# A 15 by 15 box filter's second layer: rows turned through one scaled difference instead of two products

## The reference

```python
x = x + mean_filter(group_norm(x), k=15)   # ones/15 down the rows, then ones/15 along them, zero padding of 7
```

## Time and profile before

| | us |
|---|---|
| median of 3 runs (3734.6 to 3736.6) | 3735.91 |
| the profiled execution | 3737.8 |
| its span | 3736.0 |
| TensorE busy in the span | 3338.8 (89%) |
| VectorE busy | 3140.5 (84%) |
| GpSimd busy | 2583.7 (69%) |
| ScalarE busy | 2201.5 (59%) |
| layer 1 of the second image, 914 to 1073 | 159 |

### The profile page before, as it was taken

The page is one execution under the profiler, slowest core; times in us unless marked ns, Lnnn a source line. Parts: engine busy times, 40 slices in busy tenths (PEclk is TensorE's granted clock), DMA queues, the critical chain, the costliest instruction groups (busy, mean ns, idle before and its releaser), DMA issues.

```text
span 3736.0 us, 114624 instructions
## 1 busy us (share of the span) xinstructions
PE 3338.8 (89%) x38496; PEld 2215.3 (59%) x38496; DVE 3140.5 (84%) x5910; ACT 2201.5 (59%) x4341; POOL 2583.7 (69%) x2119
## 2 busy tenths in 40 slices
PE   2199899998989989899899998999899998999978
PEld 1155476555765567555675556755576555765567
DVE  6689977998879978899788997789877998879976
ACT  2778733786248852588426883278633786248842
POOL 4089952997639965499546995389853996639964
PEclk9599999999999999999999999999999999999999
DMA  9566577664867648666485665766477664866634
GB/s 212 167 103 129 98 198 189 118 129 83 237 159 126 128 96 238 140 126 128 123 238 116 127 122 153 222 107 128 96 202 188 119 128 85 236 160 125 129 85 136
DMA packets 720201, 544.18 MB, mean 146 GB/s; under 512 B 589840, under 2 KB 665200, under 8 KB 707568
## 3 DMA queue, kind: packets, MB, share of 16 engines
q1 hardware_dynamic: 697456, 422.30, 51.5%
q10 hardware_dynamic: 22400, 117.46, 11.8%
HBM read 258.41 MB, written 148.90 MB: 109 GB/s over the span
## 4 chain that ended last, share of the span: by engine, by line
PE 77%; DVE 8%; issue 5%; ACT 4%; SPq 2%; ACTq 1%; DMA 1%; POOL 1%; DVEq 0%; POOLq 0%
PE p L581 24%; PE h_ps L693 15%; PE h_ps L491 9%; PE h_odd L491 9%; PE p L719 6%; PE p L530 5%; PE p L588 3%; PE h_ps L581 2%; DVE ob_all L1295 2%; ACT arena L762 1%; ACTq L920 1%; PE p L499 1%; PE h_ps L588 1%; SPq L413 1%; ACT ob_all L783 1%
## 5 line engine op out<-in xcount | busy, mean ns | idle before, releaser
L581 PE MATMUL p<-arena,bd_all 64*64 64x512 f16 x16896 | 1291.2, 381 | 33.2 <-DVE ob_all L1217 23.2
L1427 POOL TENSOR_TENSOR arena<-img 128x512 f32<-128x512 f32 x392 | 499.5, 1275 | 459.4 <-PE h_ps L693 437.8
L762 ACT ACTIVATE arena<-h_ps 128x512 f16<-128x512 f32 x512 | 305.8, 597 | 834.9 <-PE h_ps L693 596.3
L581 PEld LDWEIGHTS p<-arena,bd_all 64*64 64x64 f16 x16896 | 552.5, 105 | 379.5 <-issue 240.0
L1378 POOL TENSOR_TENSOR ob_all<-ob_all,img 128x512 f32<-128x512 f32 x512 | 663.5, 1296 | 91.1 <-DVE ob_all L1211 62.7
L1381 POOL TENSOR_TENSOR ob_all<-ob_all 128x512 f32<-128x512 f32 x512 | 653.4, 1276 | 40.1
L693 PE MATMUL h_ps<-bd_all,arena 128*128 128x128 f32 x3584 | 539.5, 286 | 0.0
L1279 DVE TENSOR_TENSOR arena<-h_ps,arena 128x512 f16<-128x512 f32 x512 | 353.3, 690 | 209.4 <-ACT arena L762 207.8
L693 PEld LDWEIGHTS h_ps<-bd_all,arena 128*128 128x128 f32 x3584 | 447.6, 191 | 121.2 <-issue 115.8
L1211 DVE SCALAR_TENSOR_TENSOR ob_all<-p,bias_c,cosw 128x256 f32<-128x256 f32 x1024 | 447.6, 478 | 59.8 <-PE p L581 23.0
L837 ACT ACTIVATE img<-img,half_row (+1 forms) x1024 | 486.4, 528 | 4.7
(11 more groups left out here) (177 smaller groups left out, 5050.9 us busy)
## 6 DMA issues: line engine op xcount, KB each, us to landing
out<-ob_all SPq DMA_DIRECT2D x512, 256.0 KB, 4.2
bd_all<-bd_dram SPq DMA_DIRECT2D x512, 224.0 KB, 2.6
img<-in_x ACTq DMA_DIRECT2D x168, 512.0 KB, 7.2
img<-in_x ACTq DMA_DIRECT2D x112, 256.0 KB, 4.7
img<-in_x SPq DMA_DIRECT2D x24, 512.0 KB, 25.7
bd_dram<-ob_all SPq DMA_DIRECT2D x11, 768.0 KB, 4.9
arena<-arena SPq DMA_TRANSPOSE x512, 2.8
xT_more<-arena SPq DMA_TRANSPOSE x512, 2.8
```

The lines of the kernel that those rows point to most:

```text
L581: m = mm(bank[out_half * HP:(out_half + 1) * HP, :], bd[s % RB][rows, 6 * lm + (j if own else j + 1), :], part, start=opens and i3 == 0, s ...
L1427: G.tensor_tensor(diff[u % 2], img[:, u + R, :], img[:, u - R - 1, :], ALU.subtract).then_inc(moved, 1)
```

## The change

Every row from 1 to 63 is now one difference. For u = 1 to 7 the upper neighbour's rows 57 to 63, and for u = 57 to 63 the lower neighbour's rows 0 to 6, are copied by DMA one band over into seven buffers `across` (`rows_before` and `rows_after`, issued by SyncE; the outermost band gets zeros from the table `no_row`). GpSimd subtracts for all 63 rows. ScalarE scales the difference in place (`scale_row`), with a bias for the outermost bands in the 14 border rows, and no scaled matrices are made. TensorE turns the scaled row with its transpose instruction in f32, identity as the moving operand, into one of four banks, two rows ahead of the box instead of one. `parts` and `diff` have three buffers instead of two. The waits of GpSimd's first differences are on the copies (`before_in`) and no longer on `s_scale`. `border`, `kept_row` and the product that spread the mean (line 730) are gone. A load of the next image waits for seven more differences than before.

```diff
@@ -51,7 +51,9 @@
 SCRATCH = 16
-NDIFF = T - K
+NDIFF = T - 1
+NTURN = 4
+COPIES = 5
 LAG = 16
@@ -181,10 +184,14 @@
-        diff = [piece[s] for s in range(2)]
-        parts = [piece[2 + s].bitcast(F16).rearrange("p (l k m) -> p l k m", l=2, k=NQ) for s in range(2)]
+        diff = [piece[s] for s in (0, 1, 11)]
+        parts = [piece[s].bitcast(F16).rearrange("p (l k m) -> p l k m", l=2, k=NQ) for s in (2, 3, 12)]
         head, tail = piece[14], piece[15]
-        kept_row = [piece[4 + r] for r in range(R - 1)] + [head]
+        across = [piece[4 + r] for r in range(R)]
+        across_all = arena[:, 4 * W:(4 + R) * W]
+        def diff_row(u):
+            return across[u - 1] if u <= R else diff[u % 3] if u < T - R else across[u - (T - R)]
@@ -238,7 +242,8 @@
         c_tab = h_ps[:, 1, 0:3 * P].rearrange("p (i t a) -> p i t a", i=3, a=2)
-        turned_ps = [h_ps[:, s, :].rearrange("p (k m) -> p k m", k=NQ) for s in range(2)]
+        turned_ps = [bank.rearrange("p (k m) -> p k m", k=NQ)
+                     for bank in (h_ps[:, 0, :], h_ps[:, 1, :], h_odd[:], p1[:])]
@@ -429,19 +433,49 @@
+            def rows_before(b):
+                def shifted(first, rows, signal):
+                    to, at = across_all[:, first * W:(first + rows) * W], T - R + first
+                    of = img[:, at:at + rows, :].rearrange("p t w -> p (t w)")
+                    for hl in range(HL - 1):
+                        sp.dma_start(to[hl + 1:P:HL], of[hl:P:HL]).then_inc(signal, 16)
+                    sp.dma_start(to[HP:P:HL], of[HL - 1:HP:HL]).then_inc(signal, 16)
+                sp.wait_ge(p0_ready, (b + 1) * T + PRIMED)
+                sp.dma_start(across_all[0:HP:HL], tab["no_row"]).then_inc(before_in[0], 16)
+                sp.wait_ge(x1_whole, (b + 1) * T - 3)
+                shifted(0, 4, before_in[0])
+                sp.wait_ge(x1_whole, (b + 1) * T)
+                shifted(4, 3, before_in[1])
+            def rows_after(b):
+                of = img[:, 0:R, :].rearrange("p t w -> p (t w)")
+                sp.wait_ge(turned, b * T + R + 1)
+                for hl in range(HL - 1):
+                    sp.dma_start(across_all[hl:P:HL], of[hl + 1:P:HL]).then_inc(after_in, 16)
+                sp.dma_start(across_all[HL - 1:HP:HL], of[HP:P:HL]).then_inc(after_in, 16)
+                sp.dma_start(across_all[HP + HL - 1:P:HL], tab["no_row"]).then_inc(after_in, 16)
             with sp.Fori(0, B - 1) as b:
                 matrices(b)
+                rows_before(b)
                 for j in range(T // 2):
...
                     store(b, j, j % NS)
+                    if j == 2:
+                        rows_after(b)
                     if j == 4:
...
@@ -687,27 +721,23 @@
-                def turn_row(u, *terms):
+                def turn_first():
                     for k in range(NQ):
-                        for i, (mat, row) in enumerate(terms):
-                            m = mm(turned_ps[u % 2][:, k, :], row[:, k * P:(k + 1) * P], mat,
-                                   start=(i == 0), stop=(i == len(terms) - 1))
+                        cols = slice(k * P, (k + 1) * P)
+                        mm(turned_ps[0][:, k, :], head[:, cols], tb["ident"][:], start=True, stop=False)
+                        m = mm(turned_ps[0][:, k, :], tail[:, cols], tb["prev"][:], start=False, stop=True)
                     m.then_inc(turned, 1)
...
-                    if u >= 2:
-                        pe.wait_ge(low_done, b * T + u - 1)
-                    if u <= R:
-                        turn_row(u, (turn_mat["ident"], img[:, u + R, :]),
-                                 (turn_mat["neg_prev"], img[:, u + T - R - 1, :]))
-                    elif u < T - R:
-                        pe.wait_ge(moved, b * NDIFF + u - R)
-                        turn_row(u, (turn_mat["ident"], diff[u % 2]))
-                    else:
-                        pe.wait_ge(row_kept, b * R + u - (T - R) + 1)
-                        turn_row(u, (turn_mat["next_"], kept_row[u - (T - R)]),
-                                 (turn_mat["neg_ident"], img[:, u - R - 1, :]))
+                    if u >= NTURN:
+                        pe.wait_ge(low_done, b * T + u - (NTURN - 1))
+                    pe.wait_ge(scaled_row, b * NDIFF + u)
+                    for k in range(NQ):
+                        m = nc.tensor.transpose(turned_ps[u % NTURN][:, k, :], diff_row(u)[:, k * P:(k + 1) * P],
+                                                tb["ident"][:])
+                    m.then_inc(turned, 1)
@@ -716,7 +746,7 @@
                         for l in range(2):
-                            m = mm(p0[0][:, lo:hi], parts[u % 2][:, l, k, :],
+                            m = mm(p0[0][:, lo:hi], parts[u % 3][:, l, k, :],
                                    tb["band16"][:, lo - k * P + R:hi - k * P + R],
@@ -725,15 +755,11 @@
                 pe.wait_ge(tail_ready, b + 1)
-                turn_row(0, (tb["ident"][:], head[:]), (tb["prev"][:], tail[:]))
-                pe.wait_ge(mean_made, b + 1)
-                mm(c_ps[:, 24:24 + C], sc[:, 24:25].broadcast_to([P, P]), mean_in[:], start=True, stop=True).then_inc(mean_spread, 1)
-                pe.wait_ge(mats_ready, b * 4 + 2)
+                turn_first()
+                turn_step(1)
                 for u in range(T):
-                    if u + 1 < T:
-                        if u + 1 == T - R:
-                            pe.wait_ge(mats_ready, b * 4 + 4)
-                        turn_step(u + 1)
+                    if u + 2 < T:
+                        turn_step(u + 2)
                     box_row(u)
@@ -895,35 +921,39 @@
+                def scale_row(u):
+                    act.wait_ge(moved, b * NDIFF + u)
+                    bias = edge_bias[:, 0:1] if u <= R else edge_bias[:, 1:2] if u >= T - R else None
+                    scaled(diff_row(u), diff_row(u), sc[:, 10:11], bias).then_inc(scaled_row, 1)
                 def high_part(u):
-                    if R < u < T - R or u == 0:
-                        act.wait_ge(turned, b * T + u + 1)
-                    else:
-                        act.wait_ge(bordered, b * (2 * R) + (u if u <= R else u - (T - R) + R + 1))
-                    if u >= 2:
-                        act.wait_ge(banded, b * T + u - 1)
-                    copy(parts[u % 2][:, 0], turned_ps[u % 2]).then_inc(high_done, 1)
+                    act.wait_ge(turned, b * T + u + 1)
+                    if u >= 3:
+                        act.wait_ge(banded, b * T + u - 2)
+                    copy(parts[u % 3][:, 0], turned_ps[u % NTURN]).then_inc(high_done, 1)
...
                 scaled(head, head, sc[:, 10:11], sc[:, 18:19]).then_inc(head_ready, 1)
-                scaled(turn_mat["ident"], tb["ident"][:], sc[:, 10:11]).then_inc(mats_ready, 1)
-                scaled(turn_mat["neg_prev"], tb["prev"][:], sc[:, 17:18]).then_inc(mats_ready, 1)
+                act.wait_ge(ends_ready, b + 1)
+                scale_row(1)
+                scale_row(2)
                 high_part(0)
-                scaled(turn_mat["next_"], tb["next_"][:], sc[:, 10:11]).then_inc(mats_ready, 1)
-                scaled(turn_mat["neg_ident"], tb["ident"][:], sc[:, 17:18]).then_inc(mats_ready, 1)
                 def load_next(t, rows, signal):
...
                     act.wait_ge(row_out, PRIMED + b * T + t + rows)
-                    if t + rows <= NDIFF:
-                        act.wait_ge(moved, b * NDIFF + t + rows)
+                    if t + rows + R <= NDIFF:
+                        act.wait_ge(moved, b * NDIFF + t + rows + R)
+                    if t < R:
+                        act.wait_ge(after_in, (b + 1) * (16 * COPIES))
                     for i in range(2):
...
                 for u in range(1, T):
+                    if u + 2 < T:
+                        scale_row(u + 2)
                     high_part(u)
-                    if u <= R:
-                        copy(kept_row[u - 1], img[:, u - 1, :]).then_inc(row_kept, 1)
                     if follow:
@@ -1276,16 +1306,8 @@
                     dve.wait_ge(high_done, b * T + u + 1)
-                    V.tensor_tensor(parts[u % 2][:, 1], turned_ps[u % 2], parts[u % 2][:, 0],
+                    V.tensor_tensor(parts[u % 3][:, 1], turned_ps[u % NTURN], parts[u % 3][:, 0],
                                     ALU.subtract).then_inc(low_done, 1)
-                def border(u):
-                    dve.wait_ge(turned, b * T + u + 1)
-                    first, op = (0, ALU.add) if u <= R else (HP + HL - 1, ALU.subtract)
-                    edge_cols = turned_ps[u % 2][:, :, first:first + HP - HL + 1:HL]
-                    V.tensor_tensor(edge_cols, edge_cols, mean_row[:].unsqueeze(1).broadcast_to([P, NQ, C]),
-                                    op).then_inc(bordered, 1)
@@ -1298,16 +1320,13 @@
                 V.tensor_scalar(tail, tail, sc[:, 10:11], sc[:, 23:24], ALU.mult, ALU.add).then_inc(tail_ready, 1)
```

(39 more changed lines are left out.)

18 lines of the change are left out of this document (9 added, 9 removed).

## The result

The changed kernel takes 3852.03 us (median of 4 runs, 3848.83 to 3856.55) against 3735.28 before (4 runs, 3734.6 to 3736.6): 1.0315 times as long, 95% interval 1.0302 to 1.0328. Forecast were 3607, in a range from 3540 to 3690, so a faster kernel; this one is slower.

What follows compares the result with a forecast made beforehand. TensorE was taken as the bound nearly everywhere. Savings of 9.6 + 10.5 + 0.7 - 3.5 - 2.4 = 14.9 us an image, by seven 104, plus 25.0 in the last, gave 129 off 3737.8: 3607 us, range 3540 to 3690.

Steps and rivals of the forecast that it cites:

- The step that failed: Rows 17 to 55: GpSimd, at 1.28 us a difference plus a quarter of a table product, was not the bound.
- four candidates for rows 17 to 55: Possible next bounds per row: VectorE 1.81 us, GpSimd 1.28 plus a quarter table product, ScalarE 1.69, transfers 1.83 or 1.91.
- Rival 3: Layer 1's rows: TensorE's clock falls if transpositions do not hold it up; 4180 us; 9%, plus 4% for some rows only.
- the turn at 0.53 us: TensorE's turning of a row by transposition takes 0.53 us, where the f32 product took 1.05.
- rows without sums at 1.55: Rows 0 to 17 and the last image: 1.55 us a row, 9.6 us saved in rows 0 to 17.
- the last image: Row 0 to row 63 falls from 125.1 to 97.7 us through more banks, buffers and lead; 25.0 saved after the start.
- the start 2.4 late: Before row 0: three two-input VectorE instructions computing the scale each wait 0.8 us behind GpSimd's differences, 2.4 us an image.
- rival 2: Before row 0: all small scale instructions alternate with GpSimd's differences, start 10.1 us late instead of 2.4; 3669 us; 9%.
- 1.95 us a row: Rows 17 to 55, bounded by transfers and VectorE: 74.1 us instead of 84.6, 10.5 saved an image.
- rival 4: Better than forecast: transfers reach 1.81 us a row and nothing is late, 84 us with the last image; 3523 us; 5%.
- 23.2 from the transfers and ScalarE's issues: Rows 55 to 63: 2.90 us a row from transfers (2.93) and ScalarE (some 3.1), 23.9 before, 0.7 saved.
- the 3.5 us that the transfers were to give back: End of an image: transfers need 118.7 us but the stages hold 115.2, so 3.5 us are lost again.

## Why the prediction was wrong

- **The step that failed** is "GpSimd: a difference is 1.28 us, plus a quarter of a table product. Not the bound." As a load that was right. What I left out is where the table product waits: for sums that TensorE finishes two steps before the next difference is wanted, with a difference, a scaling, high part, low part and addition still to come. Of the four candidates for rows 17 to 55 I compared durations only. 109.62 us came instead of 74.1, 35.5 of the 37 us by which the second image misses its forecast. The whole forecast was 245 us off (3852 less 3607); moving that one call gives 300.
- **Handing on.** The stall is long because it passes through two engines' orders. ScalarE's is shown (183 us by turning it round, the clock's return among them); that VectorE's `low_part` in front of the addition adds to it is read from the timeline and was not tried.
- **The load's new wait on `after_in`** I had costed at nothing, without saying so. It is 4.6 us an image, some 32 in all, and the slow clock behind it puts rows 12 to 15 2.0 us apart. Moving the copies and the loads alone returned 12.
- **Rival 3, the clock.** A low clock did come, as a consequence of the stalls: in some 120 of the 512 rows of the eight images, 23%, the box's products took over 0.9 us instead of 0.65, in none of the last image. I wrote that it would fall if transpositions did not hold it up; the last image has 1.00 with them at 67% busy, the kernel with the weights moved 1.00, and doubling them repairs it. Of the 25 us that rows 17 to 55 lost against before, doubling gave back 6 (109.62 against 103.23), although its longer turns put the rows between the stalls at 2.09. The clock's part is larger, by an estimate: ahead of the first slow products (rows 19 to 22) rows came 1.79 apart and the stalled one 4.69; three of the one and one of the other make 10.06, and 38 rows at that 95.6; so some 14 of the 25 are the clock's and 11 the stalls' own. The Trainium skill ("TensorE: Matmul & The Clock Gate", PE-mode transpose) says that transpose mode does not count as busy for the clock in the same way. These rows do not bear it out where transpositions stand between other products, since more of them alone raised the clock from 0.81 to 0.97; a stretch of nothing but transpositions was not run.
- **Nearly right**: the turn at 0.53 us (0.60 for its four instructions, 0.63 of a full row of 1.79 when the box's and the sums' 0.58 are taken off); rows without sums at 1.55 (1.56 measured); the last image (27.4 less for the rows, 26.1 measured); the start 2.4 late (1.96), and rival 2 false, since one-input instructions of one element took 0.14 to 0.15 beside GpSimd. Of the two-input form I had taken 0.8 more for each of three; the rows above show 1.14, 1.00 and 1.19 where 0.22, 0.16 and 0.16 stand without GpSimd, 0.93 more on the mean.
- **Right for another kernel**: 1.95 us a row is what the kernel before takes with the transposition alone (1.96), but that is coincidence: there the transfers' share is 0.91 (944 to 998 us), and each second box waits some 0.3 us for VectorE's addition. The changed kernel without the stall does better (1.81), which is rival 4's figure; TensorE, VectorE and transfers are all full there.
- **Terms that did not show.** With the weights moved, rows 55 to 63 take 18.29 us where I had 23.2 from the transfers and ScalarE's issues, and row 63 to the end of the sums 8.57, so the 3.5 us that the transfers were to give back are not there; they moved 319 GB/s in rows 55 to 63, more than the 289 that I took as their rate. Rival 4's sum comes to 81 us from its own terms, not 84, which changes nothing.
- **The reason for the last image** was half right. I put its gain down to banks, buffers and lead, and with f32 products it comes out the same (98.7). But in the inner rows the transposition alone in the old order gives most of it too (1.66 for the long step; the 14 border rows stay as they were, and the image gains 12 of the 26 us). Either opens the same chain; together they gain no more than the box and the addition allow.

## What to carry over

An engine far from full can still set the pace: for every wait in an engine's order write down in which step of the other engine it is released and in which step the instruction behind it is wanted, and do it again when a change alters the lead, even if that wait is not touched. Where a profile shows no engine near full and idle time in periods, look in the groups for the instruction with the largest idle time and ask what stands behind it. Before dropping a change that came out slower, move the call that waits: here one call, two rows later, turned 3% slower into 5% faster.
